# Linear attention's inputs in 128 + 64 rows: the 64-row tail kept twice, so that two tail products run on the two halves of the array

## The chip, the cores and the metric

The kernel runs on one core of one Trainium2 chip. Times are device microseconds (us) of an execution; the kernel before took 355.68 us, the median of three runs (355.44, 355.68, 358.33). One more execution was taken with the profiler.

## The reference

A small vision and text model of two layers. Sixteen items have 64 image tokens and 32 text tokens each (N = 96) of D = 192 features, 1536 tokens in all. The first layer (token projection, segmented softmax attention, a mixture of eight experts) is not touched. The part that matters is the attention of the second layer, which is linear:

```python
x = _layernorm(h)                          # (16, 96, 192)
qkv = x @ w_qkv.T                          # 192 -> 3 * 192, contraction over 192 features
q, k, v = ...                              # 12 heads of 16
q = q / max(sum_over_tokens(|q|), 1e-12);  k = k / max(sum_over_tokens(|k|), 1e-12)
kv  = einsum('bhnd,bhne->bhde', k, v)
out = einsum('bhnd,bhde->bhne', q, kv)
h = h + out @ w_proj.T + b_proj
```

A soft mixture of slots follows (norm, logits, two softmaxes, slot inputs, a small two-layer network, slot outputs) and is added to `h`, the output. All numbers are fp32.

## The kernel before

The 1536 tokens are worked on in four groups (`J` = 4) of 384 tokens (`TOK`), each of four items and three blocks (`NB` = 3) of 128 tokens; a block holds 32 tokens of each of the group's four items. Every engine has its own program, written out by hand as a list of calls such as `turn_linear(2)`; semaphores order them between engines (`sem`, and `need`, a wait whose count may be zero). PS is PSUM, eight banks of 512 fp32 columns.

The stages on PE (TensorE) are: tokens and first attention to about 119 us, experts from 128 to 252 us, then `combine`, which adds the experts' outputs to the tokens, woven with the linear attention of group 0, 1, 2 and 3 to about 320 us, woven in turn with the soft mixture, which ends the kernel.

For one group j the linear attention goes:

- DVE: `linear_moments(j)` and, after POOL has taken the power -1/2, `linear_norm(j)` write the normed tokens `xn` (semaphore `b_xn`, one count a block).
- PE: `turn_linear(j)` turns the three blocks (`flip`, line 240) into banks 0 and 1, the features in rows. The 192 features are halved: 96 in each bank. `keep_linear_inputs(j)` on ACT (line 1246) copies both banks to `xnT` (`b_xnT`).
- PE: `linear_keys_values(j, blk)` (line 754) multiplies one block of tokens by 384 columns of weights, over 2 x 96 features, into bank 2 + blk. `keep_keys_values` on ACT (line 1252) copies each bank to `kv1` (`b_kv`, one count a block).
- PE: `linear_queries(j)` (line 767) makes the queries, turned, 2 x 96 features in rows and 384 tokens in columns, in banks 0 and 1; ACT copies them (line 1259, `b_q1T`), DVE sums them (`query_norms`, line 1762) and scales them.
- PE: `key_products(j)` (line 777), `key_sums(j)` (line 792); DVE masks the products (`own_heads`, line 1786, `b_kvbd`); PE: `linear_outputs(j)` (line 803), which writes banks 1 and 2 and so waits until key block 0 of the next group has been copied (`b_kv` at 4, 7, 10); ACT copies them; PE: `linear_project(j, part)` (line 815) into banks 3 and 4; DVE: `add_linear(j, part)` (line 1793) adds to `h` (`b_h`).
- `key_products(2)` waits for `b_h` at 4, which is `add_linear(1, 1)`.

A matmul here has its weights as the stationary operand and streams the columns of the other. Some matmuls use part of the array: `combine` (line 726) multiplies into the two halves of the output rows (64 array columns each), and the experts' inner products (`expert_inner`, line 697) take 128 feature rows first and then the 64-row tail, of which `xeT` has a copy on each row half; lines 704 to 709 issue the tail matmuls of two output banks one after the other, one on each half.

SP issues the loads in the order of its program: first experts, the second layer's weights (`layer1_in`, lines 349 to 353, nine DMAs), the routes (`store_routes`, `spread_routes`), further experts. PE and ACT wait for all of `layer1_in` before the second layer.

Of the kernel before, what the change touches and what calls it, by code (L numbers as in the profile page):

```python
# [18 lines left out]
D = 192  # L19
HD = D // 2  # L20
# [11 lines left out]
TOK = NB * 128  # L32
TILES = J * NB

C1, HEADS0, HDIM0, SEGS = 96, 12, 8, 4
# [5 lines left out]
E, F = 8, 768  # L41
# [5 lines left out]
DT = D - 128  # L47
# [23 lines left out]

WP, PX = C1 + E + 1, D + 2 * E
ATTN0_DMAS = 10
LAYER1_DMAS = 9


TOK_AT = (((4, 0), (5, 0)), ((6, 0), (6, 200)), ((4, 0), (4, 200)), ((4, 0), (4, 200)))
# [12 lines left out]
def build(nc, xin, xhalo, txt, wtok, wtok2, lnw, lnb, tokbias, consts, wred, bred, wqkv0, bqkv0, wproj0, bproj0,  # L90
          wrouter, wi, wo, wq1, wkv1, wproj1, bproj1, slots, lscale, wdown, bdown, wup, bup, out):
    with ExitStack() as ctx:  # L92
        def sb(name, shape, dt=F32):
            return ctx.enter_context(nc.sbuf_tensor("sb_" + name, shape, dt))
# [3 lines left out]
        def sem(name):  # L98
            if name not in sems:
                sems[name] = ctx.enter_context(nc.semaphore(name))  # L100
            return sems[name]

        def need(eng, name, count):

            if count > 0:
                eng.wait_ge(sem(name), count)

        PS = ctx.enter_context(nc.psum_tensor("banks", [128, 8, 512], F32))
# [3 lines left out]
        def const(name, rows=128):  # L112
            a, w = CONST_AT[name]
            return cst[0:rows, a:a + w]

        ident = const("ident")
# [26 lines left out]
        w_red = sb("w_red", [HD, 2, C1 + E])  # L143
# [11 lines left out]
        dm_r = sb("dm_r", [128, NB])  # L155
        rs_r = sb("rs_r", [128, J, NB])
        xn = sb("xn", [128, NB, D])
        xnT = sb("xnT", [HD, 2, TOK])
        xrT = sb("xrT", [C1 + 1, TOK + 8])
        qT = sb("qT", [C1, TOK + 8])  # L160
        smax = sb("smax", [128, NGRP, 4 * GRP])
# [37 lines left out]
        e_out = w_space[:].rearrange("s (g e) d -> s g e d", g=PAIRS)  # L199


        w_q1 = sb("w_q1", [HD, 2, D])
        w_kv1 = sb("w_kv1", [HD, 2, 2 * D])
        w_proj1 = sb("w_proj1", [HD + 1, 2, D])
        kv1 = mid[:, 0:1152].rearrange("t (b n) -> t b n", b=NB)
        abs_k = mid[:, 1152:1152 + D]
# [33 lines left out]
        def flip(dst, src):  # L240

            rows = src.shape[0]
            return nc.tensor.transpose(dst, src, ident[0:rows, 0:rows])
# [15 lines left out]
        def _(sp):  # L259
# [26 lines left out]
            def load_first_experts():  # L286

                for piece in range(4 * NW):
                    sp.wait_ge(sem("a_sub"), 3 + 3 * piece // 4)
                    load_expert_part(piece // 4, piece % 4)  # L290
# [55 lines left out]
                        sp.dma_start(dst[64 * z:64 * (z + 1)], rows[z, m].partition_broadcast(64)).then_inc(sem(f"routes_in{m}"), 16)  # L346

            load_first_experts()
            for dst, src in [(w_q1[:], wq1), (w_kv1[:], wkv1), (w_proj1[0:HD], wproj1),
                             (w_proj1[HD:HD + 1, 0], bproj1.unsqueeze(0)), (slot_raw[:], slots),  # L350
                             (l_scale[:], lscale.partition_broadcast(HD)), (w_down[:], wdown), (b_down[:], bdown),
                             (w_up[:], wup)]:
                sp.dma_start(dst, src).then_inc(sem("layer1_in"), 16)
# [118 lines left out]
        def _(pe):  # L472
# [117 lines left out]
            def reduce_inputs(j):  # L590
                pe.wait_ge(sem("a_xnT"), j + 1)
                for kh in range(2):
                    mm = nc.tensor.matmul(PS[0:C1 + E, 0, 0:TOK], w_red[:, kh], xnT[:, kh], start=(kh == 0), stop=(kh == 1))
                mm.then_inc(sem("a_xr_ps"), 1)

            def queries(j):
# [129 lines left out]
            def combine(j, part):  # L726

                if j == 0:
                    pe.wait_ge(sem("combT"), TILES)
                elif j > 1:  # L730
                    pe.wait_ge(sem("moe_h"), 2 * j - 1 + part)
                if (j, part) == (3, 1):
                    pe.wait_ge(sem("b_knorm"), 1)
                for blk in ((0, 1), (2,))[part]:
                    for ep in range(E // 2):
                        if j == 0:
                            pe.wait_ge(sem("e_out"), 8 * ep + 8)
                        for hf in range(2):
                            rows = slice(64 * hf, 64 * hf + 64)
                            mm = nc.tensor.matmul(PS[rows, comb_bank(j, part), blk % 2 * D:(blk % 2 + 1) * D],  # L740
                                                  combT[:, NB * j + blk, ep, rows], e_out[:, 2 * j + hf, ep],
                                                  start=(ep == 0), stop=(ep == E // 2 - 1), skip_group_check=True)
                mm.then_inc(sem("moe_ps"), 1)


            def turn_linear(j):
                need(pe, "b_q1T", j)
                for blk in range(NB):
                    pe.wait_ge(sem("b_xn"), NB * j + blk + 1)
                    for kh in range(2):  # L750
                        mm = flip(PS[0:HD, kh, blk * 128:(blk + 1) * 128], xn[:, blk, kh * HD:(kh + 1) * HD])
                mm.then_inc(sem("b_xnT_ps"), 1)

            def linear_keys_values(j, blk):
                pe.wait_ge(sem("b_xnT"), j + 1)

                if j == 0 and blk < 2:
                    pe.wait_ge(sem("moe_h"), 2 - blk)
                need(pe, "b_kvbd", j)
                if j == 2 and blk > 0:  # L760
                    pe.wait_ge(sem("b_h"), blk)
                for kh in range(2):
                    mm = nc.tensor.matmul(PS[:, 2 + blk, 0:2 * D], xnT[:, kh, blk * 128:(blk + 1) * 128],  # L763
                                          w_kv1[:, kh], start=(kh == 0), stop=(kh == 1))
                mm.then_inc(sem("b_kv_ps"), 1)

            def linear_queries(j):
                pe.wait_ge(sem("b_xnT"), j + 1)
                need(pe, "b_kvbd", (0, 2, 0, 0)[j])
                need(pe, "b_o1T", (0, 0, 2, 3)[j])  # L770
                for mh in range(2):
                    for kh in range(2):
                        mm = nc.tensor.matmul(PS[0:HD, mh, 0:TOK], w_q1[:, kh, mh * HD:(mh + 1) * HD], xnT[:, kh],
                                              start=(kh == 0), stop=(kh == 1))
                mm.then_inc(sem("b_q_ps"), 1)

            def key_products(j):
# [25 lines left out]
            def linear_outputs(j):  # L803
                pe.wait_ge(sem("b_kvbd"), j + 1)
                pe.wait_ge(sem("b_qs"), 2 * j + 2)
                need(pe, "b_kv", (4, 7, 10, 0)[j])
                need(pe, "b_xnT", (0, 3, 0, 0)[j])
                for mh in range(2):
                    for b in range(4):
                        dst = PS[0:HD, 1 + mh, 0:TOK].rearrange("k (x b t) -> k b x t", x=NB, b=4)[:, b]  # L810
                        src = q1T[:, mh].rearrange("k (x b t) -> k b x t", x=NB, b=4)[:, b]
                        mm = nc.tensor.matmul(dst, kv_bd[:, b, mh], src, start=True, stop=True)
                mm.then_inc(sem("b_oT_ps"), 1)
# [102 lines left out]
            patches(2, 1)  # L916
            free(a_xnT=1)
            reduce_inputs(0)
            square_rows(2)
            queries(0)  # L920
# [18 lines left out]
            patches(3, 0)  # L939
            free(a_xnT=2)  # L940
            reduce_inputs(1)
            patches(3, 1)
            square_sums(3)
# [25 lines left out]
            weigh_values(0, 2)  # L969
            free(a_xnT=3)  # L970
            reduce_inputs(2)
            free(a_oT=1)
            project(0)
# [85 lines left out]

            pe.wait_ge(sem("layer1_in"), 16 * LAYER1_DMAS)  # L1060
            combine(0, 0)
# [5 lines left out]
            linear_keys_values(0, 0)  # L1067
            linear_queries(0)
            linear_keys_values(0, 1)
            linear_keys_values(0, 2)  # L1070
            turn_linear(1)
            combine(2, 1)
            key_products(0)
# [1 line left out]
            combine(3, 0)  # L1075
            linear_keys_values(1, 0)
            linear_keys_values(1, 1)
            linear_keys_values(1, 2)
            linear_outputs(0)
            combine(3, 1)  # L1080
            key_products(1)
# [3 lines left out]
            turn_linear(2)  # L1085
            linear_project(0, 1)
            linear_keys_values(2, 0)
            linear_keys_values(2, 1)
            linear_outputs(1)
            linear_keys_values(2, 2)  # L1090
            linear_queries(2)
            key_sums(2)
            turn_soft(0)
# [5 lines left out]
            soft_inputs(0)  # L1099
            linear_keys_values(3, 0)  # L1100
            linear_keys_values(3, 1)
            linear_keys_values(3, 2)
            linear_outputs(2)
            turn_soft(1)
            linear_project(2, 0)
# [32 lines left out]
        def _(act):  # L1138
# [22 lines left out]
            def keep_inputs(j):  # L1161
                act.wait_ge(sem("a_xnT_ps"), j + 1)
                need(act, "a_xr_ps", j)
                nc.scalar.copy(xnT[:], PS[0:HD, 0:2, 0:TOK]).then_inc(sem("a_xnT"), 1)

            def keep_reduced(j):
                act.wait_ge(sem("a_xr_ps"), j + 1)
# [78 lines left out]
            def keep_linear_inputs(j):  # L1246
                act.wait_ge(sem("b_xnT_ps"), j + 1)
                need(act, "b_q_ps", j)
                need(act, "b_kv_ps", NB * j)
                nc.scalar.copy(xnT[:], PS[0:HD, 0:2, 0:TOK]).then_inc(sem("b_xnT"), 1)  # L1250

            def keep_keys_values(j, blk):
                if blk == 0:
# [134 lines left out]
            for e in range(E):  # L1388
                keep_hidden(e)
            act.wait_ge(sem("layer1_in"), 16 * LAYER1_DMAS)  # L1390
            keep_linear_inputs(0)
# [48 lines left out]
        def _(ve):  # L1440
# [238 lines left out]
            def slot_norms():  # L1679
                ve.wait_ge(sem("layer1_in"), 16 * LAYER1_DMAS)  # L1680
                ve.tensor_tensor(slot_sq[:], slot_raw[:], slot_raw[:], ALU.mult).then_inc(sem("slot_step"), 1)
# [485 lines left out]
```

## Time and profile before

| what | value |
|---|---|
| median of 3 runs | 355.68 us |
| profiled execution, its own time | 356.81 us |
| its span in the profile | 354.7 us |
| PE busy | 334.7 us, 94% |
| DVE busy | 203.0 us, 57% |
| ACT busy | 97.6 us, 28% |
| granted clock of TensorE | full in all slices |
| PE, line 763 (keys and values) | 48 instructions |
| PE, line 773 (queries) | 32 instructions |

Busy times are those of one profiled execution. PE's matmuls are pipelined: the time from the start of one to the start of the next says what it costs, and its recorded duration is longer. In a timeline a line stands for a run of like instructions: its start, its length to the modelled end of the last one, and how many they are; a length thus contains the tail of the last instruction, which the next line overlaps. A matmul on fp32 data is recorded as two instructions, a `flip` as one. Idle time is put down to what ended it.

### The profile page before, as it was taken

Reading aid. Unit: us, or ns where it says so; the run is one execution under the profiler, and the core shown is the slowest. Engines: PE = TensorE matmul, PEld = TensorE weight load, DVE = VectorE, ACT = ScalarE, POOL = GpSimd, SP = SyncE. Lnnn points to the kernel's source line nnn. Section 1 sums busy time; section 2 is a strip of 40 time slices with the busy share of each in tenths; the row PEclk is TensorE's granted clock in tenths of the full one; section 3 lists DMA queues with packets and bytes.
Section 4 is the critical chain, followed back from the end, with each engine's and each line's share of the span. In section 5 each row is a group of like instructions: output and inputs, shape, how many; then the busy total and the mean of one; then the engine's idle time right before and its main releaser. Section 6 shows DMA issues by size and latency. Waiting matters only on the chain. (4 is left out here: it accounts for less than half of the span.)

```text
span 354.7 us, 8688 instructions
## 1 busy us (share of the span) xinstructions
PE 334.7 (94%) x3672; PEld 240.3 (68%) x3672; DVE 203.0 (57%) x639; ACT 97.6 (28%) x188; POOL 40.7 (11%) x87
## 2 busy tenths in 40 slices
PE   3999999999999989999999999999999989899895
PEld 3776566867767437595866859586876766776665
DVE  3926487789897964124324332432354456969864
ACT  1224555665552431011010100101012213332250
POOL 8603331110102020000000000000020011101100
PEclk9999999999999999999999999999999999999999
DMA  7946002314160006999199240000000000000005
GB/s 259 344 111 226 2 6 68 107 36 122 24 164 3 2 8 143 188 196 217 44 206 196 60 133 0 3 0 0 2 2 0 2 0 3 3 0 2 0 2 133
DMA packets 28194, 26.74 MB, mean 75 GB/s; under 512 B 4506, under 2 KB 23324, under 8 KB 28156
## 3 DMA queue, kind: packets, MB, share of 16 engines
q1 hardware_dynamic: 27260, 25.60, 29.2%
q10 hardware_dynamic: 896, 0.59, 0.7%
q8 instruction: 29, 0.48, 0.6%
q14 instruction: 9, 0.07, 0.1%
HBM read 24.91 MB, written 1.28 MB: 74 GB/s over the span
## 5 line engine op out<-in xcount | busy, mean ns | idle before, releaser
L720 PEld LDWEIGHTS banks<-sb_wo_sl,sb_attn_hidT_attn 128*128 128x128 f32 x384 | 62.2, 190 | 5.6 <-issue 4.9
L720 PE MATMUL banks<-sb_wo_sl,sb_attn_hidT_attn 128*128 128x192 f32 x384 | 64.5, 328 | 0.0
L1732 DVE COPY sb_w_tok_e_out<-banks 60x384 f32<-60x384 f32 x32 | 17.8, 555 | 49.8 <-PE banks L720 49.3
L1242 ACT ACTIVATE sb_attn_hidT_attn<-banks 128x480 f32<-128x480 f32 x24 | 13.7, 572 | 102.8 <-PE banks L707 102.8
L702 PE MATMUL banks<-sb_tok_xeT,sb_wi_sl 128*128 128x480 f32 x96 | 40.1, 567 | 1.1 <-ACT sb_tok_xeT L1227 1.1
L1722 DVE TENSOR_SCALAR sb_attn_hidT_attn<-banks 128x480 f32<-128x480 f32 x24 | 15.8, 658 | 27.8 <-PE banks L707 25.9
L702 PEld LDWEIGHTS banks<-sb_tok_xeT,sb_wi_sl 128*128 128x128 f32 x96 | 18.0, 190 | 18.9 <-issue 17.0
L486 PE MATMUL banks<-sb_tok_xeT 128*32 128x193 f32 (+1 forms) x512 | 24.8, 328 | 0.7 <-DMA sb_tok_xeT<-in_xhalo 0.7
L486 PEld LDWEIGHTS banks<-sb_tok_xeT 128*32 128x32 f32 (+1 forms) x512 | 17.1, 109 | 6.6 <-issue 4.0
L707 PE MATMUL banks<-sb_tok_xeT,sb_wi_sl 64*128 64x480 f32 x96 | 21.5, 580 | 0.0
L740 PE MATMUL banks<-sb_w_tok_e_out,sb_onehot_combT 128*64 128x192 f32 x192 | 16.9, 329 | 0.1
L763 PE MATMUL banks<-sb_w_kv,sb_xnT 96*128 96x384 f32 x48 | 16.8, 493 | 0.2 <-ACT sb_xnT L1250 0.2
L707 PEld LDWEIGHTS banks<-sb_tok_xeT,sb_wi_sl 64*128 64x128 f32 x96 | 8.6, 186 | 12.3 <-issue 12.3
L740 PEld LDWEIGHTS banks<-sb_w_tok_e_out,sb_onehot_combT 128*64 128x64 f32 x192 | 13.2, 137 | 2.7 <-DVE sb_w_tok_e_out L1732 0.5
L1499 DVE BATCH_NORM_STATS2 sb_stat<-sb_h 128x6 f32<-128x192 f32 x48 | 14.0, 348 | 0.3
L457 POOL MEMSET sb_attn_hidT_attn<- 1x384 f32 x1 | 0.4, 413 | 119.6 <-PE banks L720 119.6
L613 PE MATMUL banks<-sb_w_v,sb_xrT 97*32 97x96 f32 x512 | 13.2, 248 | 0.5 <-issue 0.5
L1146 ACT ACTIVATE sb_onehot_combT<-sb_tok_xeT 128x1024 f32<-128x1024 f32 x8 | 8.5, 1058 | 18.4 <-DMA sb_tok_xeT<-in_xhalo 18.3
L642 PEld LDWEIGHTS banks<-sb_attn_hidT_attn 128*32 128x32 f32 x384 | 11.9, 113 | 1.6 <-ACT sb_attn_hidT_attn L1208 0.9
L763 PEld LDWEIGHTS banks<-sb_w_kv,sb_xnT 96*128 96x128 f32 x48 | 8.7, 190 | 6.1 <-issue 0.7
L503 PE MATMUL banks<-sb_w_tok_e_out,sb_ln_b 128*128 128x192 f32 x30 | 7.5, 411 | 5.5 <-DMA sb_w_tok_e_out<-in_wtok 5.5
L642 PE MATMUL banks<-sb_attn_hidT_attn 128*32 128x24 f32 x384 | 12.5, 190 | 0.2
(236 smaller groups left out, 533.8 us busy)
## 6 DMA issues: line engine op xcount, KB each, us to landing
sb_wo_sl<-in_wo SPq DMA_DIRECT2D x16, 288.0 KB, 3.6
sb_tok_xeT<-in_xin SPq DMA_DIRECT2D x8, 448.0 KB, 5.5
sb_onehot_combT<-route_rows SPq DMA_DIRECT2D x6, 512.0 KB, 8.8
sb_wi_sl<-in_wi SPq DMA_DIRECT2D x8, 288.0 KB, 3.2
sb_wi_sl<-in_wi SPq DMA_DIRECT2D x24, 96.0 KB, 3.2
sb_xn<-route_rows SPq DMA_DIRECT2D x4, 512.0 KB, 11.3
sb_w_tok_e_out<-in_wtok SPq DMA_DIRECT2D x2, 960.0 KB, 6.8
sb_attn_hidT_attn<-route_rows SPq DMA_DIRECT2D x2, 512.0 KB, 12.1
```

The source lines that it names most:

```text
L486: nc.tensor.matmul(PS[QB * b:QB * b + QB, bank, at:at + D + 1], x_k[0:rows, (2 * j + b // 2) % NX, t, cols], w_eff[0:rows, t], start=(t == ...
L613: mm = nc.tensor.matmul(PS[32 * r:32 * r + 32, V_BANK[b % 2], s * C1:(s + 1) * C1], xrT[:, at:at + 32], w_v4[:, r], start=True, stop=True)
L642: mm = nc.tensor.matmul(PS[g * 32:g * 32 + 32, 3, at:at + SEG], v_exp[:, j % 2, b, s, g * 32:g * 32 + 32], probT[:, g, b, s * 32:s * 32 + ...
L702: nc.tensor.matmul(PS[:, HID_BANKS[f], 0:SLOTS], wi_sl[:, q, f * 128:(f + 1) * 128], xeT[:, 0, e].rearrange("k g c -> k (g c)"), start=Tru ...
L707: nc.tensor.matmul(PS[:, HID_BANKS[2 * n + z], 0:SLOTS], wi_sl[rows, q, F + n * 128:F + (n + 1) * 128], xeT[rows, 1, e].rearrange("k g c - ...
L720: mm = nc.tensor.matmul(PS[:, 4 + j // 2, j % 2 * D:(j % 2 + 1) * D], hidT[:, e % 2, f, j * 128:(j + 1) * 128], wo_sl[:, q, f], start=(f = ...
L740: mm = nc.tensor.matmul(PS[rows, comb_bank(j, part), blk % 2 * D:(blk % 2 + 1) * D], combT[:, NB * j + blk, ep, rows], e_out[:, 2 * j + hf ...
L763: mm = nc.tensor.matmul(PS[:, 2 + blk, 0:2 * D], xnT[:, kh, blk * 128:(blk + 1) * 128], w_kv1[:, kh], start=(kh == 0), stop=(kh == 1))
L1242: nc.scalar.activation(hidT[:, e % 2, f].rearrange("f (g c) -> f g c", g=PAIRS)[:, :, 0:CAP], PS[:, HID_BANKS[f], 0:SLOTS].rearrange("f (g ...
L1499: ve.bn_stats(stat6[:, blk], h[:, j, blk]).then_inc(sem("stat6"), 1)
L1722: ve.tensor_scalar(hidT[:, e % 2, f].rearrange("f (g c) -> f g c", g=PAIRS)[:, :, 0:CAP], PS[:, HID_BANKS[f], 0:SLOTS].rearrange("f (g c) ...
L1732: ve.tensor_copy(e_out[64 * (e % 2):64 * (e % 2) + CAP, hf * 4 + z:hf * 4 + z + 3:2, e // 2], PS[64 * z:64 * z + CAP, 4 + hf, 0:2 * D].rea ...
```

## The change

`xnT` and the weights `w_q1` and `w_kv1` have 128 rows in place of 96. Their first slot holds features 0 to 127, their second features 128 to 191 twice, in rows 0 to 63 and in rows 64 to 127. The turn makes the first slot with one flip a block and writes the tail into both halves of the rows with two matmuls by the identity. A key block or a half of the queries is then one product over 128 rows and one over 64; the tail products of key blocks 0 and 1, and those of the two halves of the queries, are issued one after the other on different row halves and into different banks. Key blocks 0 and 1 are made in one call (part 0), block 2 in another (part 1). For group 2, `linear_outputs(1)` stands after part 0 and before part 1. The weights come in 15 DMAs in place of 9. The first layer uses the first 96 rows of `xnT` as before.

```diff
-LAYER1_DMAS = 9
+LAYER1_DMAS = 15
-        xnT = sb("xnT", [HD, 2, TOK])
+        xnT = sb("xnT", [128, 2, TOK])
-        w_q1 = sb("w_q1", [HD, 2, D])
-        w_kv1 = sb("w_kv1", [HD, 2, 2 * D])
+        w_q1 = sb("w_q1", [128, 2, D])
+        w_kv1 = sb("w_kv1", [128, 2, 2 * D])
...
             load_first_experts()
-            for dst, src in [(w_q1[:], wq1), (w_kv1[:], wkv1), (w_proj1[0:HD], wproj1),
+            for dst, src in [(w_kv1, wkv1), (w_q1, wq1)]:
+                sp.dma_start(dst[0:HD, 0], src[:, 0]).then_inc(sem("layer1_in"), 16)
+                sp.dma_start(dst[HD:128, 0], src[0:128 - HD, 1]).then_inc(sem("layer1_in"), 16)
+                for z in range(2):
+                    sp.dma_start(dst[z * DT:(z + 1) * DT, 1], src[128 - HD:, 1]).then_inc(sem("layer1_in"), 16)
+            for dst, src in [(w_proj1[0:HD], wproj1),
...
                 for blk in range(NB):
                     pe.wait_ge(sem("b_xn"), NB * j + blk + 1)
-                    for kh in range(2):
-                        mm = flip(PS[0:HD, kh, blk * 128:(blk + 1) * 128], xn[:, blk, kh * HD:(kh + 1) * HD])
+                    cols = slice(blk * 128, (blk + 1) * 128)
+                    flip(PS[:, 0, cols], xn[:, blk, 0:128])
+                    for z in range(2):
+                        mm = nc.tensor.matmul(PS[z * DT:(z + 1) * DT, 1, cols], xn[:, blk, 128:D], ident, start=True, stop=True)
                 mm.then_inc(sem("b_xnT_ps"), 1)
 
-            def linear_keys_values(j, blk):
+            def linear_keys_values(j, part):
                 pe.wait_ge(sem("b_xnT"), j + 1)
 
-                if j == 0 and blk < 2:
-                    pe.wait_ge(sem("moe_h"), 2 - blk)
+                if j == 0 and part == 0:
+                    pe.wait_ge(sem("moe_h"), 2)
                 need(pe, "b_kvbd", j)
-                if j == 2 and blk > 0:
-                    pe.wait_ge(sem("b_h"), blk)
-                for kh in range(2):
-                    mm = nc.tensor.matmul(PS[:, 2 + blk, 0:2 * D], xnT[:, kh, blk * 128:(blk + 1) * 128],
-                                          w_kv1[:, kh], start=(kh == 0), stop=(kh == 1))
-                mm.then_inc(sem("b_kv_ps"), 1)
+                if j == 2:
+                    pe.wait_ge(sem("b_h"), part + 1)
+                blocks = ((0, 1), (2,))[part]
+                for blk in blocks:
+                    nc.tensor.matmul(PS[:, 2 + blk, 0:2 * D], xnT[:, 0, blk * 128:(blk + 1) * 128], w_kv1[:, 0],
+                                     start=True, stop=False)
+                for blk in blocks:
+                    rows = slice(blk % 2 * DT, (blk % 2 + 1) * DT)
+                    nc.tensor.matmul(PS[:, 2 + blk, 0:2 * D], xnT[rows, 1, blk * 128:(blk + 1) * 128], w_kv1[rows, 1],
+                                     start=False, stop=True).then_inc(sem("b_kv_ps"), 1)
 
             def linear_queries(j):
...
                 for mh in range(2):
-                    for kh in range(2):
-                        mm = nc.tensor.matmul(PS[0:HD, mh, 0:TOK], w_q1[:, kh, mh * HD:(mh + 1) * HD], xnT[:, kh],
-                                              start=(kh == 0), stop=(kh == 1))
+                    nc.tensor.matmul(PS[0:HD, mh, 0:TOK], w_q1[:, 0, mh * HD:(mh + 1) * HD], xnT[:, 0], start=True, stop=False)
+                for mh in range(2):
+                    rows = slice(mh * DT, (mh + 1) * DT)
+                    mm = nc.tensor.matmul(PS[0:HD, mh, 0:TOK], w_q1[rows, 1, mh * HD:(mh + 1) * HD], xnT[rows, 1],
+                                          start=False, stop=True)
                 mm.then_inc(sem("b_q_ps"), 1)
...
             linear_project(0, 1)
             linear_keys_values(2, 0)
+            linear_outputs(1)
             linear_keys_values(2, 1)
-            linear_outputs(1)
-            linear_keys_values(2, 2)
             linear_queries(2)
...
-                nc.scalar.copy(xnT[:], PS[0:HD, 0:2, 0:TOK]).then_inc(sem("b_xnT"), 1)
+                nc.scalar.copy(xnT[:], PS[:, 0:2, 0:TOK]).then_inc(sem("b_xnT"), 1)
```

For the other groups `linear_keys_values(j, 2)` is dropped from PE's list, and the first layer's product and copy name `xnT[0:HD]`.

## Rows read from the trace of the kernel before

**Rows 1.** The page: busy time, share of the span and instructions of each engine.

```profile
PE 334.7 (94%) x3672; PEld 240.3 (68%) x3672; DVE 203.0 (57%) x639; ACT 97.6 (28%) x188; POOL 40.7 (11%) x87
```

**Rows 2.** Timeline of PE, last expert: start, length, line, operation, shapes, count.

```profile
236.54 4.99 PE L702 MATMUL banks<-sb_tok_xeT,sb_wi_sl 128*128 128x480 f32 x12
241.46 2.69 PE L707 MATMUL banks<-sb_tok_xeT,sb_wi_sl 64*128 64x480 f32 x12
244.08 8.07 PE L720 MATMUL banks<-sb_wo_sl,sb_attn_hidT_attn 128*128 128x192 f32 x48
252.08 8.35 PE L740 MATMUL banks<-sb_w_tok_e_out,sb_onehot_combT 128*64 128x192 f32 x96
```

**Rows 3.** Timeline of PE, the linear attention, with idle time ahead in brackets.

```profile
260.36 0.86 PE L243 MATMUL banks<-sb_cst,sb_xn 128*96 128x128 f32 x6
261.15 2.82 PE L740 MATMUL banks<-sb_w_tok_e_out,sb_onehot_combT 128*64 128x192 f32 x32
263.90 1.56 PE L763 MATMUL banks<-sb_w_kv,sb_xnT 96*128 96x384 f32 x4
265.29 2.74 PE L773 MATMUL banks<-sb_xnT,sb_w_q 96*96 96x384 f32 x8
267.87 2.74 PE L763 MATMUL banks<-sb_w_kv,sb_xnT 96*128 96x384 f32 x8
270.45 0.82 PE L243 MATMUL banks<-sb_cst,sb_xn 128*96 128x128 f32 x6
271.20 1.52 PE L740 MATMUL banks<-sb_w_tok_e_out,sb_onehot_combT 128*64 128x192 f32 x16
272.65 1.27 PE L787 MATMUL banks<-sb_attn_hidT_attn 32*96 32x96 f32 x48
...
286.52 2.79 PE L773 MATMUL banks<-sb_xnT,sb_w_q 96*96 96x384 f32 x8 [0.90 <-DVE sb_attn_hidT_attn L1790]
...
290.45 0.82 PE L243 MATMUL banks<-sb_cst,sb_xn 128*96 128x128 f32 x6
291.11 0.82 PE L824 MATMUL banks<-sb_w_proj,sb_attn_hidT_attn 97*128 97x192 f32 x4
292.16 2.85 PE L763 MATMUL banks<-sb_w_kv,sb_xnT 96*128 96x384 f32 x8 [0.23 <-ACT sb_xnT L1250]
294.84 1.52 PE L812 MATMUL banks<-sb_attn_hidT_attn 96*96 96x96 f32 x16
...
301.84 1.47 PE L824 MATMUL banks<-sb_w_proj,sb_attn_hidT_attn 97*128 97x192 f32 x8
...
305.75 1.27 PE L787 MATMUL banks<-sb_attn_hidT_attn 32*96 32x96 f32 x48 [1.12 <-DVE sb_h L1799]
...
317.41 2.74 PE L773 MATMUL banks<-sb_xnT,sb_w_q 96*96 96x384 f32 x8
319.99 0.17 PE L799 MATMUL banks<-sb_qmask,sb_attn_hidT_attn 128*96 128x4 f32 x1
```

**Rows 4.** Timeline of ACT: the copy of a key block behind its product.

```profile
295.04 0.48 ACT L1257 COPY sb_attn_hidT_attn<-banks 128x384 f32<-128x384 f32 x1 [0.73 <-PE banks L763]
```

**Rows 5.** Timeline of DVE, groups 1 to 3: query sums, additions to h.

```profile
301.13 1.01 DVE L1765 TENSOR_REDUCE sb_den<-sb_attn_hidT_attn 96x4 f32<-96x384 f32 x2 [1.83 <-ACT sb_attn_hidT_attn L1262]
...
303.86 0.54 DVE L1796 TENSOR_TENSOR sb_h<-sb_h,banks 128x384 f32<-128x384 f32 x1
...
305.26 0.35 DVE L1799 TENSOR_TENSOR sb_h<-sb_h,banks 128x192 f32<-128x192 f32 x1
...
321.02 1.01 DVE L1765 TENSOR_REDUCE sb_den<-sb_attn_hidT_attn 96x4 f32<-96x384 f32 x2 [0.32 <-ACT sb_attn_hidT_attn L1262]
```

**Rows 6.** Timeline of SP: DMA issues of the second layer's weights and the next ones.

```profile
98.14 0.43 SPq L353 DMA_DIRECT2D sb_w_kv<-in_wkv  x1
...
101.17 0.42 SPq L353 DMA_DIRECT2D sb_w_up<-in_wup  x1
129.97 2.59 SPq L330 DMA_DIRECT2D route_rows<-sb_routes_t  x4
```

More of the change, by code:

```diff
@@ L592, in reduce_inputs @@
                 for kh in range(2):
-                    mm = nc.tensor.matmul(PS[0:C1 + E, 0, 0:TOK], w_red[:, kh], xnT[:, kh], start=(kh == 0), stop=(kh == 1))
+                    mm = nc.tensor.matmul(PS[0:C1 + E, 0, 0:TOK], w_red[:, kh], xnT[0:HD, kh], start=(kh == 0), stop=(kh == 1))
                 mm.then_inc(sem("a_xr_ps"), 1)
@@ L1069, in _ @@
             linear_keys_values(0, 1)
-            linear_keys_values(0, 2)
             turn_linear(1)
@@ L1077, in _ @@
             linear_keys_values(1, 1)
-            linear_keys_values(1, 2)
             linear_outputs(0)
@@ L1101, in _ @@
             linear_keys_values(3, 1)
-            linear_keys_values(3, 2)
             linear_outputs(2)
@@ L1163, in keep_inputs @@
                 need(act, "a_xr_ps", j)
-                nc.scalar.copy(xnT[:], PS[0:HD, 0:2, 0:TOK]).then_inc(sem("a_xnT"), 1)
+                nc.scalar.copy(xnT[0:HD], PS[0:HD, 0:2, 0:TOK]).then_inc(sem("a_xnT"), 1)
             def keep_reduced(j):
```

## The prediction

> **What bounds the kernel now.** I read the page's busy shares first, then the timeline of each engine over the stage that the change touches, and last the neighbouring stages for phases of TensorE that look like the new ones. PE is busy 94% of the span, DVE 57%, ACT 28% [rows 1]. The stage of the change runs from 260.36 us, where the linear attention's first inputs are turned, to the first query products of the last group, 317.41 to 319.99 us [rows 3]. PE runs there almost without a gap: the gaps that decide something are 0.90 us before the queries of group 1, 0.23 before the keys of group 2, 1.12 before the key products of group 2 [rows 3]. So a microsecond more or less on PE moves the end, except where a DVE chain is about as long. From about 321 us on a chain over DVE, ACT and PE sets the end, and nothing in it is edited: it only starts earlier or later.
>
> **The grain of PE.** A matmul is two instructions here, a flip one. 384 columns take 0.3225 us each (8 in 2.58, 265.29 to 267.87), 128 columns about 0.109 (six flips in 0.66, 290.45 to 291.11) [rows 3]. Below, a "slot" is one matmul of 384 columns, 0.645 us.
>
> **What running side by side costs.** The experts already do what the change does. Twelve full instructions of 480 columns take 4.92 us (236.54 to 241.46), 0.4025 each and 0.09 over; twelve on half the rows take 2.62 (241.46 to 244.08), which is six times 0.4025 plus 0.20 [rows 2]. So pairs do run side by side, but each stretch on half rows costs 0.09 on the way in, 0.105 for first weights that nothing hides and 0.095 on the way out, and the full instruction behind it again has bare first weights: 48 outer instructions take 8.00 us (244.08 to 252.08) for 48 times 0.1625, again 0.20 over (0.105 first weights, 0.09 out) [rows 2]. I call a change of array shape a switch: 0.093 us of emptying plus first weights of 0.105 (128 columns), 0.08 (96), 0.05 (64 columns or a flip). The last figures: 32 instructions in column halves take 2.75 us for 16 times 0.1625, 0.15 over, 16 take 1.45, also 0.15 over; six flips between two of those stretches take 0.79 against 0.66 with full shapes around them [rows 3]. Against this, 96 rows followed by 96 columns (263.90, 265.29) is no switch: both are the full shape.
>
> The Trainium skill (TensorEngine Tiling (Array Packing), Key Properties) says that changing the tiling mode drains the engine, and gives no price. By it the sum is mine below, 359.0 us; by that page's gain for small dimensions alone it would be the first rival's, 352.5. The trace agrees with the drain.
>
> **Part by part, PE's own time.**
> - *Turning, `turn_linear`.* Before, six flips. After, per block: one flip of 128 columns (full shape), then two matmuls into column halves, four instructions in two levels. The shape alternates with every block. A lone flip costs 0.109 + 0.05 + 0.093 = 0.25; a tail stretch 2 x 0.109 + 0.05 + 0.093 = 0.36; a block 0.61. Groups 0 and 1 stand after another shape and before a combine that has the tail's shape, so that the last emptying and the combine's first weights fall away: 3 x 0.25 + 2 x 0.36 + 0.27 = 1.75, against 0.79 + 0.05 and 0.75 + 0.05: **+0.91 and +0.95**. Groups 2 and 3 stand among full shapes: 0.20 for the first flip, 2 x 0.25, 3 x 0.36, and 0.105 for the next weights make 1.89, against 0.66: **+1.24 each**. The trace has no phase of one instruction. Bounds: no bare weights for the lone flip, 0.20, or the full recorded length of a first flip in a new shape, about 0.31, plus 0.093, so 0.40. I take 0.25, since the first flip at 260.36 behaves so. Over the flips that lie on the path (some nine) the bounds are -0.5 and +1.4 us.
> - *Keys and values.* Six slots become three full, one pair and one alone. Blocks 0 and 1: 4 x 0.3225 + 0.093 + 0.105 + 2 x 0.3225 + 0.093 = 2.23, against 2.58. Block 2: its half-row matmul has no partner and still forces the switches: 0.645 + 0.093 + 0.105 + 0.645 + 0.093 = 1.58, against 1.29, and 0.105 more where it follows another shape (all but group 2). Together with 0.08 at what follows: about **+0.12** for groups 1 and 3.
> - *Queries.* Four slots become two full and a pair: 1.29 + 0.093 + 0.08 + 0.645 = 2.11 until the products are there, against 2.58, then 0.093 and first weights for the next: **-0.47** for who waits for the queries, about **-0.28** for PE.
> - *Group 0* has keys, queries, block 2 in one row: 2.23 + 2.28 + 1.69 = 6.19 against 6.45: **-0.26**.
> - *A new wait.* The outputs of group 1 need the copy of key block 0 of group 2 out of its bank (b_kv at 7). Before, block 1 stood between, two slots. After, block 0 is ready only together with block 1. ACT starts 0.20 us after the stream ends (294.84 to 295.04) and takes 0.48 [rows 4]: outputs 0.73 us after the stream instead of 0.093, **+0.64**, with the bound 0 if the last columns are released earlier. Queued behind it on PE: block 2, queries, everything. The outputs of groups 0 and 2 have block 2's 1.6 us in front and don't wait.
> - *Hidden.* ACT's copy of 128 instead of 96 partitions has the same columns. Six more DMAs on SP cost 6 x 0.43 to 0.65 = 2.6 to 4 us after 101.6 us; SP's next work comes at 129.97 us, when the routes are ready [rows 6], and PE wants the weights at 252 us. If that cover were gone, the routes would be 4 us late. `reduce_inputs` is untouched in size.
>
> **The sum along the path** (shift of PE against before). Turn 0 +0.91, group 0 -0.26, turn 1 +0.95: 1.60. Keys 1 +0.12: 1.72; the wait before the queries of group 1 shifts with it, since it hangs on the combine just before. Queries 1 -0.28: 1.44. Turn 2 +1.24, of which the gap before the keys of group 2 takes back 0.20 (it waits for ACT's copy of the turned inputs, not for PE): 2.48. Keys 2, blocks 0 and 1, -0.35; new wait +0.64; block 2 +0.29: 3.06. Queries 2, with 0.08 for their first weights: their products come at +2.67. From there DVE is busy without a gap from 301.13 to 305.6 us, and its `add_linear` of group 1 starts at 303.86, some 0.5 us after its projection was done (301.84 + 1.47) [rows 3, 5]. Turn 3 delays that projection by 1.27 beyond the chain, of which 0.5 is this slack, so that the key products of group 2, which wait for the last `add_linear` [rows 3, 5], come at 2.67 + 0.77 = +3.44; the 1.12 us gap in front of them hides the rest of turn 3. Keys 3 +0.12: 3.56. Queries 3 would give back 0.47, but DVE waits only 0.32 us for them at 321.02 [rows 5]: 3.24. From there the tail is as before, in the same order, and nothing else comes late.
>
> The profiled execution took 356.81 us (span 354.7 and 2.1 around it), 1.1 above the median of the runs, 355.68. Its sum is 356.81 + 3.2 = 360.1; on the median **359.0 us**, 0.9% slower. What this kernel can tell from no change is about 1%, so the borders are 352.1 and 359.2.
>
> **Rivals.**
> 1. *The switches cost little, pairs are pure gain (6%).* Place: every stretch on half rows and each turn. For it: the pairs at 241.46 do start together. Against: 0.20 us over in every such stretch. Price: keys -0.645 four times, queries -0.645 three times and -0.32 in group 3; turns +0.33 three times (three flips of 0.109 and six levels of 0.109 less six flips), the fourth in DVE's slack; new wait +0.64. That is -3.2: 352.5 us. The Trainium skill (TensorEngine Tiling (Array Packing), Theoretical Speedup) gives "Up to 2×" for a dimension of at most 64, which would be this rival. It decides if a switch costs under about 0.06 us in place of 0.14 to 0.2, for there the turns and the pairs cancel.
> 2. *Short phases cost more (15%).* A lone flip at 0.40, and column tails of 128 columns that don't overlap fully (+0.22 a block, as four single instructions): 1.4 + some 1.5: 361.9 us. For it: nothing like it is in the trace. Against: the pairs of 192 columns keep full overlap, 16 levels in 2.75 us [rows 3].
> 3. *Switches as priced, but hidden waits take them (12%).* The copy of block 0 comes in time and the bare weights are hidden in one-instruction phases: 3.3 - 0.64 - 0.5 = +2.1: 357.8 us.
> 4. *The layout change itself doesn't pair* (3%): half-row matmuls of different banks issued one by one add 0.645 for each of eight pairs, less slack, some +4.5 more: 363.5 us. The experts' pairs speak against it.
>
> The forecast has 64%. **Range** 356.9 to 361.4: from below rival 3 to most of rival 2, leaving out rivals 1 and 4 and some of 2. **Chances**: faster by over 1% 0.03 (only a rival 1 that undercuts its own price), slower by over 1% 0.42 (rivals 2 and 4 whole and over a third of the forecast, whose value lies 0.2 us under the border), within 1% 0.55.
>
> **What would show it.** In the new trace: each block of a turn 0.6 us long, one flip and four instructions of 64 columns; turns of 1.75 to 1.9 us; a half-row stretch of the keys 0.85 us for two levels of 0.3225; outputs of group 1 preceded by a PE gap of 0.6 us ended by ACT's key copy; key products of group 2 with a smaller gap than 1.12; the tail from DVE's query sums of group 3 to the end as long as before. I am wrong in the mechanism if consecutive phases of different shape follow each other at 0.109 or 0.3225 us, and in the size if a lone flip isn't near 0.25 us.

## The result and the profile after

The changed kernel took 359.06 us (median of 15 runs) where the kernel before took 355.70 in the same 15: +3.36 us, a ratio of 1.0097 with a 95% interval of 1.0067 to 1.0126. Forecast were 359.0 us and a range of 356.9 to 361.4. The profiled execution took 359.46 us, its span is 357.3 (before 354.7).

| stage, by PE's starts in the trace | before | after |
|---|---|---|
| up to the first expert product | 128.33 | 127.38 |
| experts and first combines, to the first turn | 132.03 | 132.02 |
| linear attention, first flip of group 0 to the key sums of group 3 | 59.63 | 63.34 |
| from there to the end of the span | 34.67 | 34.56 |

The third row is where the change shows: **+3.71 us**. The first stage has the same work but for SP's six further loads and differs by 0.95 us between the two executions. After, e1, e4, e6 and e9 have exactly the same code there, and their first expert product starts between 126.30 and 128.07 us; over all traces of this study the range is 126.3 to 129.3 us. The second and fourth rows move by no more than 0.01 and 0.2 us. So from here on I read two things for each kernel: the ratio over all runs, and the length of this one stage in its trace, which is free of the first stage's scatter.

The page after, which answers to [rows 1]: PE's busy time is 3.2 us longer, DVE's is the same.

```profile
PE 337.9 (95%) x3708; PEld 236.7 (66%) x3708; DVE 203.0 (57%) x639; ACT 97.3 (27%) x188; POOL 41.0 (11%) x87
```

Timeline of PE in the trace after, group 0, then the stretch of group 2 and the keys of group 3 (start, length to the modelled end, line, shapes, count); it answers to [rows 3]:

```profile
259.40 0.33 PE L243 MATMUL banks<-sb_cst,sb_xn 128*128 128x128 f32 x1
259.66 0.44 PE L758 MATMUL banks<-sb_cst,sb_xn 128*64 128x128 f32 x4
260.03 0.33 PE L243 MATMUL banks<-sb_cst,sb_xn 128*128 128x128 f32 x1
...
261.19 2.77 PE L745 MATMUL banks<-sb_w_tok_e_out,sb_onehot_combT 128*64 128x192 f32 x32
263.89 1.56 PE L771 MATMUL banks<-sb_w_kv,sb_xnT 128*128 128x384 f32 x4
265.38 0.92 PE L775 MATMUL banks<-sb_w_kv,sb_xnT 64*128 64x384 f32 x4
266.22 1.53 PE L783 MATMUL banks<-sb_xnT,sb_w_q 128*96 128x384 f32 x4
267.68 0.89 PE L786 MATMUL banks<-sb_xnT,sb_w_q 64*96 64x384 f32 x4
268.50 0.91 PE L771 MATMUL banks<-sb_w_kv,sb_xnT 128*128 128x384 f32 x2
269.35 0.91 PE L775 MATMUL banks<-sb_w_kv,sb_xnT 64*128 64x384 f32 x2
270.19 0.33 PE L243 MATMUL banks<-sb_cst,sb_xn 128*128 128x128 f32 x1
...
291.01 0.27 PE L243 MATMUL banks<-sb_cst,sb_xn 128*128 128x128 f32 x1
291.21 0.44 PE L758 MATMUL banks<-sb_cst,sb_xn 128*64 128x128 f32 x4
...
293.81 1.56 PE L771 MATMUL banks<-sb_w_kv,sb_xnT 128*128 128x384 f32 x4
295.30 0.92 PE L775 MATMUL banks<-sb_w_kv,sb_xnT 64*128 64x384 f32 x4
297.05 1.57 PE L825 MATMUL banks<-sb_attn_hidT_attn 96*96 96x96 f32 x16 [0.84 <-ACT sb_attn_hidT_attn L1266]
...
308.76 1.27 PE L800 MATMUL banks<-sb_attn_hidT_attn 32*96 32x96 f32 x48 [0.66 <-DVE sb_h L1808]
...
311.35 1.46 PE L771 MATMUL banks<-sb_w_kv,sb_xnT 128*128 128x384 f32 x4
312.73 0.92 PE L775 MATMUL banks<-sb_w_kv,sb_xnT 64*128 64x384 f32 x4
```

The turn of group 0 now reads as flip, tail, flip, tail, flip, tail: a flip that streams 0.109 us holds PE 0.26 (259.40 to 259.66), four tail instructions in two levels hold it 0.37, and the turn lasts 1.79 us where it took 0.79. The pair of key tails (265.38 to 266.22) takes 0.84 for two levels of 0.3225; the tail of block 2 alone (269.35 to 270.19) takes the same 0.84 for half the work. Before the outputs of group 1 there is a gap of 0.84 that was not there, ended by ACT's copies of key blocks 0 and 1 (timeline of ACT, after, answers to [rows 4]):

```profile
296.32 0.86 ACT L1266 COPY sb_attn_hidT_attn<-banks 128x384 f32<-128x384 f32 x2 [2.56 <-PE banks L775]
```

On DVE (timeline after, answers to [rows 5]) the addition of group 1 now waits for its projection, and the query sums of group 3 start without idle time behind the operation ahead:

```profile
303.29 1.01 DVE L1774 TENSOR_REDUCE sb_den<-sb_attn_hidT_attn 96x4 f32<-96x384 f32 x2 [1.79 <-ACT sb_attn_hidT_attn L1271]
...
306.82 0.55 DVE L1805 TENSOR_TENSOR sb_h<-sb_h,banks 128x384 f32<-128x384 f32 x1 [0.71 <-PE banks L837]
...
323.66 0.16 DVE L1816 TENSOR_SCALAR sb_soft_stat<-sb_mv_s 128x3 f32<-128x3 f32 x1
323.73 1.00 DVE L1774 TENSOR_REDUCE sb_den<-sb_attn_hidT_attn 96x4 f32<-96x384 f32 x2
```

SP (timeline after, answers to [rows 6]) issued the fifteen loads from 96.71 to 105.10 us, 8.39 us where the nine took 3.93 (97.66 to 101.59), and was still done 24 us before its next work:

```profile
96.71 0.43 SPq L350 DMA_DIRECT2D sb_w_kv<-in_wkv  x1
...
104.67 0.43 SPq L358 DMA_DIRECT2D sb_w_up<-in_wup  x1
129.02 2.60 SPq L330 DMA_DIRECT2D route_rows<-sb_routes_t  x4
```

### The profile page after: what moved, and what is told of

It is laid out like the page before. It is cut to its first block and busy times, and to the rows that moved or that the text cites. A ratio compares the mean times of both kernels' runs of the same rounds, so it can differ in the third digit from the quotient of the medians.

```text
span 357.3 us, 8762 instructions
## 1 busy us (share of the span) xinstructions
PE 337.9 (95%) x3708; PEld 236.7 (66%) x3708; DVE 203.0 (57%) x639; ACT 97.3 (27%) x188; POOL 41.0 (11%) x87
## 5 line engine op out<-in xcount | busy, mean ns | idle before, releaser
L618 PEld LDWEIGHTS banks<-sb_w_v,sb_xrT 97*32 97x32 f32 x512 | 10.7, 110 | 2.3 <-issue 1.1
L243 PE MATMUL banks<-sb_cst,sb_attn_hidT_attn 128*128 128x128 f32 (+1 forms) x72 | 10.5, 279 | 1.5 <-DVE sb_h L1595 1.0
```

The source lines that it names most:

```text
L618: mm = nc.tensor.matmul(PS[32 * r:32 * r + 32, V_BANK[b % 2], s * C1:(s + 1) * C1], xrT[:, at:at + 32], w_v4[:, r], start=True, stop=True)
```

## The experiments

All edits are to the changed kernel unless said otherwise. Each ratio is against runs of the kernel before on the same chip; it is taken over all runs and is not the quotient of the two medians, from which it differs by up to 0.0017. A "stage" is the third row of the table above, in the one trace of each kernel.

| kernel | median us | ratio to before, 95% interval | stage in its trace |
|---|---|---|---|
| before | 355.5 to 356.3 by set of runs | 1 | 59.63 |
| after | 359.06 | 1.0097 (1.0067 to 1.0126) | 63.34 |
| e1 turn regrouped | 356.69 | 1.0029 (1.0003 to 1.0056) | 60.92 |
| e2 tails doubled by DVE | 355.60 | 0.9965 (0.9935 to 0.9996) | 59.66 |
| e3 turn alone | 360.62 | 1.0135 (1.0104 to 1.0165) | 63.85 |
| e4 no pairs | 363.22 | 1.0212 (1.0183 to 1.0241) | 67.80 |
| e5 block 2 over all rows | 358.09 | 1.0071 (1.0043 to 1.0099) | 61.89 |
| e6 outputs later | 359.34 | 1.0110 (1.0069 to 1.0151) | 63.64 |
| e7 three edits | 354.08 | 0.9945 (0.9926 to 0.9965) | 58.54 |
| e8 one visit | 354.27 | 0.9958 (0.9937 to 0.9980) | 58.19 |
| e9 block 0 alone | 358.87 | 1.0073 (1.0046 to 1.0100) | 62.69 |
| e10 all edits | 353.12 | 0.9905 (0.9873 to 0.9937) | 57.42 |

One thing lies outside all stages. In the kernels in which DVE writes the tails twice (e2, e7, e8, e10) an execution is 1.8 to 1.9 us longer than its span in the profile, in all the others 2.1 to 2.2. These four therefore gain some 0.3 us in the medians that no stage shows; the cause is not known.

### e1: the same turn, one change of shape

```diff
-                    flip(PS[:, 0, cols], xn[:, blk, 0:128])
-                    for z in range(2): ...tail matmuls of this block
+                for blk in range(NB): flip(...)          # three flips
+                for blk in range(NB): ...tail matmuls    # then six tails
```

> The changed kernel with the turn's work regrouped: first the three flips, then all six tail matmuls. Same instructions, one change of shape where there were three round trips. Theory (a change of array shape costs 0.093 us of emptying plus 0.05 of bare weights): each turn loses two round trips, 4 x 0.143 = 0.57 to 0.62 us; all four turns lie on the path now (DVE waits 0.71 us for the projection behind the fourth), so -2.3 to -2.5 us, 356.7 us. Rival (the tail matmuls themselves are the cost, four instructions of two passes where a flip was one): no change, 359.1 us.

Measured 356.69 us and a stage of 60.92, 2.42 under after. Timeline of PE in e1, the first turn:

```profile
260.09 0.55 PE L243 MATMUL banks<-sb_cst,sb_xn 128*128 128x128 f32 x3
260.57 0.88 PE L759 MATMUL banks<-sb_cst,sb_xn 128*64 128x128 f32 x12
261.27 2.77 PE L745 MATMUL banks<-sb_w_tok_e_out,sb_onehot_combT 128*64 128x192 f32 x32
```

The same fifteen instructions take 1.18 us in place of 1.79 (259.40 to 261.19). Nothing but the order differs, with one change of shape inside where there were five. So the order alone costs 0.61 us a turn, 0.15 us for each of the four changes that are gone. In this edit each change of shape is also a change between a flip and a matmul. The flips of the kernel before speak against that as the cause: six of them between matmuls over the full array take 0.66 us (290.45 to 291.11 in [rows 3]), 6 x 0.109 and next to nothing over, and the eight matmuls ahead of them take 1.30 us (289.15 to 290.45), which is 8 x 0.1625. Timeline of PE in before, ahead of those flips:

```profile
289.15 1.47 PE L824 MATMUL banks<-sb_w_proj,sb_attn_hidT_attn 97*128 97x192 f32 x8
```

### e2: the change without its turn, e3: the turn without the rest

e2 lets DVE write the tail features a second time, so that two flips of 128 columns turn a block:

```diff
+                ve.tensor_copy(xn[:, :, D:], xn[:, :, 128:D]).then_inc(sem("b_xn"), 1)   # DVE
...
+                for a in range(2):
+                    for blk in range(NB):
+                        mm = flip(PS[:, a, blk * 128:(blk + 1) * 128], xn[:, blk, 128 * a:128 * (a + 1)])
```

> The changed kernel with the old turn's cost: DVE writes the 64 tail features a second time beside the normed tokens (one copy of 3 x 64 columns a group), and PE turns each block with two flips of 128 columns, no change of shape. Keys, values and queries stay as changed. Theory (the loss sits in the turns, +3.9 us along the path by the two traces, and the pairs with their switches and the new wait come out a little under zero): 359.1 - 3.9 + 0.1 for the copy in front of the first turn = 355.3 us, level with the kernel before. Rival (the half-row stretches and the new wait are the loss): 358 us or more.

e3 keeps the turn and makes the second half of the tail's weights zero, with `rows = slice(0, 128)` in keys and queries:

> The other half alone: the changed turn, but keys, values and queries multiply all tails over 128 rows, the second half of the tail's weights being zero, so that no product runs side by side and none changes the shape; ten slots a group as in the kernel before. Theory: before plus the turns, 355.7 + 3.9, and 0.3 for the outputs of group 1, whose key block is now ready one matmul before the stretch ends and not two: 359.9 us. Rival (the pairs and their switches are the loss): 356.5 us or less.

e2: 355.60 us, a stage of 59.66, 3.68 under after and level with before; the interval of its ratio ends just under 1, which the 0.3 us outside the span can explain. e3: 360.62 us, a stage of 63.85, 4.22 over before. In e3 the rows around the outputs of group 1 show the short wait that was expected (timeline of PE in e3):

```profile
294.55 1.56 PE L772 MATMUL banks<-sb_w_kv,sb_xnT 128*128 128x384 f32 x4
295.94 1.45 PE L776 MATMUL banks<-sb_w_kv,sb_xnT 128*128 128x384 f32 x4
297.60 1.57 PE L826 MATMUL banks<-sb_attn_hidT_attn 96*96 96x96 f32 x16 [0.20 <-ACT sb_attn_hidT_attn L1267]
```

Without that wait the outputs would start 1.29 us behind the tails (295.94), at 297.23; they start at 297.60, so the wait is 0.37 of e3's 4.22. Both sides agree: the turn costs 3.7 to 3.9 us of the stage, keys, queries and the new wait together about nothing. That nothing is a balance: after is 0.51 under e3, although its wait is 0.54 longer (0.91, worked out below under "The new wait"), so by this estimate the half-row products save about 1.05 us net of their changes of shape, and the wait takes most of that back.

### e4: the pairs one after the other

```diff
-                    rows = slice(blk % 2 * DT, (blk % 2 + 1) * DT)     # and mh * DT for the queries
+                    rows = slice(0, DT)
```

> The changed kernel with all tail products on row half 0, so that the same matmuls with the same switches run one after the other. Theory (pairs fully overlap): one slot, 0.645 us, more for each of eight pairs, less about 0.6 for the wait before the outputs of group 1, whose key block is ready earlier: +4.5 us, 363.5 us. Rival (pairs gain nothing): 359.1 us.

Measured 363.22 us, a stage of 67.80: +4.46. Eight pairs at 0.645 are 5.16, and the gap before the outputs of group 1 shrinks from 0.84 to 0.20. Timeline of PE in e4:

```profile
296.78 1.55 PE L775 MATMUL banks<-sb_w_kv,sb_xnT 64*128 64x384 f32 x4
298.54 1.57 PE L825 MATMUL banks<-sb_attn_hidT_attn 96*96 96x96 f32 x16 [0.20 <-ACT sb_attn_hidT_attn L1266]
```

The four tail instructions are modelled to last 1.55 us here and 0.92 after, and by starts the same stretch in group 0 holds PE 1.49 us (264.30 to 265.79) where it took 0.84 after, 0.65 more: the pairs do overlap fully. In this respect the change got what it wanted.

### e5: the tail without a partner

```diff
+        w_kvz = sb("w_kvz", [128, 2 * D])      # tail's weights in rows 0 to 63, zeros below
-                    nc.tensor.matmul(..., xnT[rows, 1, ...], w_kv1[rows, 1], ...)
+                    nc.tensor.matmul(..., xnT[:, 1, ...], w_kvz[:], ...)      # key block 2 only
```

> The changed kernel, except that the tail of key block 2, which has no partner, is multiplied over all 128 rows with weights whose second half is zero (one more small DMA, one clearing on POOL long before). Theory (a half-row matmul without a partner gains nothing and pays two changes of shape): 0.29 us less in each group plus 0.05 to 0.08 at what follows, all on the path: -1.4 us, 357.7 us. Rival (the switches around block 2 hide behind the copies on ACT or the DVE chains): 359.1 us.

The stage is 61.89, 1.45 under after, as expected; the medians differ by 0.97 us (358.09 against 359.06), within what the intervals of the two ratios allow. A product over 128 rows, half of them zeros, is cheaper here than one over 64 rows without a partner: timeline of PE in e5,

```profile
268.39 0.91 PE L774 MATMUL banks<-sb_w_kv,sb_xnT 128*128 128x384 f32 x2
269.14 0.81 PE L779 MATMUL banks<-sb_w_kvz,sb_xnT 128*128 128x384 f32 x2
269.79 0.27 PE L244 MATMUL banks<-sb_cst,sb_xn 128*128 128x128 f32 x1
```

0.65 us for the tail (269.14 to 269.79) where it took 0.84, and 0.75 in place of 0.84 for the full product ahead of it.

### e6: a miss, and where the wait went

```diff
             linear_keys_values(2, 0)
-            linear_outputs(1)
             linear_keys_values(2, 1)
+            linear_outputs(1)
...                                            # ACT's two copies likewise
```

> The changed kernel with the outputs of group 1 behind both key parts of group 2 (ACT's two copies swapped alike), so that the copy they wait for is covered by block 2. Theory (the new wait, 0.84 us in the trace after, is on the path): -0.8 us, 358.3 us. Rival (ACT or DVE then delivers the later copies late, and the gap only moves): 359.1 us.

Measured 359.34 us and a stage of 63.64, 0.3 *over* after. The outputs start at once, but the queries of group 2, which come next, now wait (timeline of PE in e6):

```profile
296.32 0.91 PE L775 MATMUL banks<-sb_w_kv,sb_xnT 64*128 64x384 f32 x2
297.15 1.60 PE L825 MATMUL banks<-sb_attn_hidT_attn 96*96 96x96 f32 x16
299.73 1.50 PE L783 MATMUL banks<-sb_xnT,sb_w_q 128*96 128x384 f32 x4 [0.98 <-ACT sb_attn_hidT_attn L1276]
```

The outputs are written to banks 1 and 2, the queries to 0 and 1, so the queries need ACT's copy of the outputs (`b_o1T` at 2). Block 2 stood between the two and covered that copy. I had looked at what waits before the moved call and not at what waits behind it.

### e7 and e8: edits together

> The tails written twice by DVE (no change of shape in the turns), key block 2 over all rows, and the outputs of group 1 behind both key parts. Theory: the three gains add, since each was on PE with the path: before - 0.6 - 1.4 - 0.8 = 2.8 us under the kernel before in the same runs, a ratio of 0.992. Rival (once PE is 3 us quicker the DVE chains of groups 2 and 3 bound): no more than 1.5 us under it.

> The kernel of the three edits, and for group 0 the key tails of blocks 0 and 1 and the query tails stand in one stretch on half rows (full products of keys and queries first). Theory (one round trip of shape less, 0.093 + 0.105 + 0.093 + 0.08 = 0.37 us): 0.3 to 0.4 us less than the three edits. Rival (the copy of the keys, now ready with the queries' tails close behind, delays the queries' copy on ACT and with it the second turn): no gain.

e7 took 354.08 us, 1.44 under the median before in the same runs, and a stage of 58.54, 1.09 under before: not 2.8, a miss. Its ratio of 0.9945 has an interval that lies above the forecast 0.992. Of the 1.7 us that the stage misses, 1.1 is e6's edit, which moves a wait and costs 0.3 where it was put down at -0.8; the other 0.6 is e2's edit, whose stage is level with before and whose 0.6 was read from the medians. The rival's number, no more than 1.5 us under before, came true, but its cause, a binding DVE chain, isn't needed: 59.66 of e2, less 1.45 of e5, plus 0.30 of e6, is 58.51. e8, with one stretch on half rows for keys and queries of group 0, has a stage of 58.19, 0.35 under e7 as forecast; the medians, 354.27 and 354.08, can't tell the two apart.

### e9: another block without a partner

```diff
+            # group 2: block 0 (full, tail alone), block 1 full | linear_outputs(1) | block 2 full, tails of 1 and 2 as the pair
+            # ACT: copy of block 0, copy of the outputs, copies of blocks 1 and 2
```

> The changed kernel, but in group 2 key block 0 is the one without a partner and blocks 1 and 2 make the pair: block 0, the full product of block 1, the outputs of group 1, the full product of block 2, the pair of tails. Same products and same number of changes of shape as after; the copy of block 0 is covered by block 1's full product (0.093 + 0.105 + 0.645 us), and the copy of the outputs, which the queries wait for, by block 2 and the pair. Theory (0.84 us of waiting is on the path, and the run with the outputs moved behind both parts gained nothing only because the queries then waited 0.98 us for the copy of those outputs): -0.7 us, 358.4 us, and both gaps under 0.2 us. Rival (a wait of this size is taken back by the DVE chain behind the queries anyway): 359.1 us, with a larger gap before the key products of group 2.

Measured 358.87 us, and a stage of 62.69: 0.65 under after, with no gap of note before the outputs and none before the queries (timeline of PE in e9):

```profile
294.99 0.91 PE L788 MATMUL banks<-sb_w_kv,sb_xnT 64*128 64x384 f32 x2
295.82 0.91 PE L785 MATMUL banks<-sb_w_kv,sb_xnT 128*128 128x384 f32 x2
296.74 1.57 PE L843 MATMUL banks<-sb_attn_hidT_attn 96*96 96x96 f32 x16
298.15 0.84 PE L785 MATMUL banks<-sb_w_kv,sb_xnT 128*128 128x384 f32 x2
298.92 0.92 PE L793 MATMUL banks<-sb_w_kv,sb_xnT 64*128 64x384 f32 x4
```

The gap before the key products of group 2 is 0.66 as after, so nothing was given back on DVE. The wait was on the path. In the medians 0.65 us is lost in the scatter: the intervals of e9 and after overlap.

### e10: a version under both

> Tails written twice by DVE, lone key tails over all rows, one stretch for the tails of group 0, and group 2 with block 0 first (its tail over all rows) as in the run before. From the kernel of the three edits, whose stage of linear attention took 58.54 us in its trace against 59.63 before: -0.35 for the one stretch, -0.98 for the gap before the queries of group 2, +0.1 for what is left of waits: a stage of 57.3 us, 2.3 us under before, a ratio of 0.9935. Rival (the DVE chain behind the queries of group 2 takes part of it back): a stage of 58 us or more.

Measured **353.12 us, ratio 0.9905 (0.9873 to 0.9937)**, a stage of 57.42, 2.21 under before. It beats both kernels. The stage accounts for a ratio of 0.9938; the median lies 0.7 us lower than that. Some 0.3 of it is the time outside the span, which is shorter in this kernel as in e2; the rest the stage doesn't explain and the scatter of the first stage may. The gap before the outputs is down to 0.20, and that before the key products of group 2 back at 1.10 (timeline of PE in e10):

```profile
293.22 0.81 PE L787 MATMUL banks<-sb_w_kv,sb_xnT 128*128 128x384 f32 x2
294.23 1.57 PE L863 MATMUL banks<-sb_attn_hidT_attn 96*96 96x96 f32 x16 [0.20 <-ACT sb_attn_hidT_attn L1303]
...
305.11 1.27 PE L838 MATMUL banks<-sb_attn_hidT_attn 32*96 32x96 f32 x48 [1.10 <-DVE sb_h L1847]
```

## Why the prediction was right, step by step

- **Turns.** Forecast 1.75 us for groups 0 and 1, measured 1.79 and 1.78; forecast for the lone flip 0.25 of bounds 0.20 to 0.40, measured 0.26 (0.20 where the shape ahead was full, 291.01 to 291.21); tail stretch forecast 0.36, measured 0.37. Groups 2 and 3, forecast 1.89 with the next weights, measured 1.83 and 0.09 behind it. e1 shows that the order is the cost, e2 and e3 that the turns are all of the loss: 3.7 to 3.9 us of the stage.
- **Keys, values and queries.** A pair 0.84 us, forecast 0.093 + 0.645 + 0.105. Keys 0 and 1 of group 1 with block 2: 277.75 to 281.77 is 4.02 against 3.97; with the outputs behind them, which pay first weights, it is 5.55 against 5.43, the forecast +0.12. Right, and e4 and e5 show both halves of it, full overlap for a pair and a loss for a single.
- **The new wait** is the term that was mis-sized: forecast +0.64, measured +0.91. The stream ended at about 296.05 (295.30 + two levels and their bare weights), and the outputs came 1.00 behind it, at 297.05, in place of 0.093. ACT started 0.27 after the stream, not 0.20, its copy took 0.48, and PE's first instruction came 0.25 after that, where I had 0.05. The gap of 0.84 in the row is shorter because it counts from the modelled end of the last tail, 296.22. e9 gives its worth on the path, 0.65 of the 0.91; its outputs still start 0.17 later than they would without a wait (296.74 against 295.82 + 0.75).
- **The path through DVE.** Forecast: the projection behind the fourth turn late by 1.27, 0.5 of it slack, 0.77 on the path. Measured: DVE waited 0.71 there, the delay grew by 0.85 from the query sums of group 2 (3.12, counted from the first turn) to the key products (3.97), and the gap before them went from 1.12 to 0.66. The queries of group 3 gave back 0.32 by the forecast and 0.42 by the trace (DVE's addition of group 2 is 4.09 late, its query sums of group 3 are 3.67 late): the 0.32 of idle time, and 0.1 because the sums now start before the recorded end of the operation ahead (323.66 + 0.16).
- **The sum** was 3.24; the same point in the trace, the query sums of group 3, came 2.71 later in an execution that was 0.96 ahead where the stage starts: 3.67. Of the 0.43 between them 0.27 is the wait, and 0.13 had gathered before it, mostly in the three turns (the keys of group 2 start 2.61 late, forecast 2.48); the small rest lies behind. Over all runs the difference is 3.36, between the two. That the median came out at 359.06 against a forecast of 359.0 is in part luck: the sum was 0.4 too small for the stage, and the difference of the medians, with an interval of some 1 us either way, happens to lie 0.35 under the stage's 3.71.
- **Hidden work.** The six further loads cost SP 4.5 us where 2.6 to 4 were forecast, and were hidden all the same; the tail after the stage is unchanged (34.56 against 34.67).
- **Rivals.** The first (switches nearly free) is out by e1 and e5, the fourth (no pairing) by e4. The second's lone flip of 0.40 and half-overlapped tails aren't there; its price was also too small by its own figures, since nine blocks on the path at +0.22 are 2.0 and not 1.5. The third's hidden waits aren't there either: e9 shows the wait on the path. Here a change of shape cost about 0.09 us of emptying and 0.05 to 0.105 of bare weights. The two parts can be told apart in the keys: four full instructions ahead of a half-row stretch, 1.29 by their columns, hold PE 1.38 where the shape ahead of them was full (311.35 to 312.73), and 1.49 where it was not (263.89 to 265.38). The Trainium skill (TensorEngine Tiling (Array Packing), Key Properties) states that TensorE drains when the tiling mode changes; the traces of after and e1 agree, and the page gives no price.

## What to carry to other kernels

Count the changes of array shape, not only the slots that pairs save: a pair of half-row products saves one product's time and pays two switches of some 0.15 to 0.2 us. Here a product was 0.645 us, so a pair was worth it; putting two stretches together saved another 0.35 (e8); one product without a partner was cheaper over zeros in the full shape (e5). From these figures I estimate that a pair in a stretch of its own stops paying where a product takes less than about 0.4 us; no run tried that. If data must lie on both row halves, and the engine that writes it has time, let it write it twice and keep the turn in one shape; here that cost DVE, 57% busy, one copy of 0.29 us a group (e2). And before a call is moved past another, look at what both neighbours' waits were covered by it.

## What the runs showed of the hardware

- A product over 128 rows of which 64 are zeros costs 0.65 us where the same product over 64 rows, alone between full shapes, holds PE for 0.84 (e5).
- Between the end of a copy on ACT and the first instruction on PE that waited for it, 0.25 us passed at the outputs of group 1 (296.80 to 297.05; the same 0.25 in e9 and e10), 0.14 at the queries in e6 (299.59 to 299.73), and 0.05 at the keys of group 2 before (292.11 to 292.16 in [rows 3]). The number of waits that follow the one in question doesn't order them: one follows at the outputs and at the keys, none at the queries. The cause is open.
- The stage in front of the change scattered by 1.8 us between the five traced executions with identical code there (126.30 to 128.07) and by 3 us over all (126.30 to 129.28), while the unchanged stages behind it repeated to 0.2 us or better. For an effect of under 1 us the length of the stage in the trace told more than the medians of 6 to 12 runs.
